# A layer with attention and routed experts: three edits to the order of its instructions

## What is computed

```python
xn = layernorm(x)                                  # no weights
qkv = xn @ W_qkv                                   # 32 query heads, 16 key/value heads of 64
scores = q @ k.T / 8 + slope[h] * (kpos - qpos)    # ALiBi, causal
s = (softmax(scores) @ v) @ W_out                  # back to width 128
logits = xn @ gate_w + gate_b                      # 8 experts, the best 2 of each token
h = gelu(xn @ w1[e] + b1[e])                       # 512 wide, exact gelu
y = sum(softmax(top2)[e] * (h @ w2[e] + b2[e]))    # over the token's two experts
out = x + s * silu(y)
```

## Time and profile before

| | us |
|---|---|
| median of 3 executions | 1218.92 |
| profiled execution | 1220.46 |
| its span, first to last instruction | 1218.7 |
| busy: PE / DVE / ACT / POOL | 1128.5 / 990.2 / 936.7 / 887.8 |
| first half (C0 of body 0 to C0 of body 31) | 55.49 to 557.33 |
| second half from C0 of body 32 | 710.32 |

### The profile page before, as it was taken

One profiled execution on the slowest core, in us unless ns is written; L12 is line 12 of the kernel. 1 busy time (PEld: TensorE's weight loads), 2 busy tenths in 40 slices (PEclk: granted clock), 3 DMA queues, 4 the chain that ended last, 5 costly groups with the idle time before them and its releaser, 6 DMA issues.

```text
span 1218.7 us, 51693 instructions
## 1 busy us (share of the span) xinstructions
PE 1128.5 (93%) x16970; PEld 833.0 (68%) x16970; DVE 990.2 (81%) x3099; ACT 936.7 (77%) x1835; POOL 887.8 (73%) x1064
## 2 busy tenths in 40 slices
PE   2668999999999999999998889999999999999996
PEld 1446666677777777777887657777777777777774
DVE  7787888878888888885776768888888888888883
ACT  4547887878888888887665578888888888888884
POOL 6059988888888888886000048888888888888895
PEclk8579999999999999999999999999999999999998
DMA  8425755655555555556335355555555555555554
GB/s 258 161 53 102 132 127 120 135 116 130 131 127 128 129 127 128 130 133 101 87 90 107 74 137 126 124 127 123 122 122 123 120 122 124 125 124 122 122 122 71
DMA packets 267956, 148.74 MB, mean 122 GB/s; under 512 B 173154, under 2 KB 256450, under 8 KB 267204
## 3 DMA queue, kind: packets, MB, share of 16 engines
q1 hardware_dynamic: 263476, 138.72, 51.3%
q0 software_dynamic: 4096, 8.40, 2.3%
q10 hardware_dynamic: 272, 0.13, 0.0%
HBM read 15.76 MB, written 16.78 MB: 27 GB/s over the span
## 4 chain that ended last, share of the span: by engine, by line
PE 64%; POOL 16%; issue 6%; DVE 4%; ACT 2%; DMA 1%; SPq 1%; POOLq 0%; ACTq 0%; DVEq 0%
POOL t_lo L812 11%; PE ps L965 10%; PE ps L937 7%; PE ps L871 7%; PE ps L872 6%; PE ps L873 6%; PE outs L997 6%; PE ps L969 5%; PE outs L1001 5%; PE outs L999 5%; PE ps L966 3%; PE ps L974 2%; ACT stage L1266 1%; POOL y_now L806 1%; PE outs L872 1%
## 5 line engine op out<-in xcount | busy, mean ns | idle before, releaser
L812 POOL TENSOR_TENSOR t_lo<-stage 128x512 f16<-128x512 f32 x640 | 652.2, 1038 | 120.4 <-ACT stage L1266 118.6
L1548 DVE CUSTOM_DVE_ANT_0 stage<-ps,kmask 128x512 bf16<-128x512 f32 (+3 forms) x1024 | 451.7, 487 | 111.0 <-PE ps L937 96.9
L1266 ACT ACTIVATE stage<-ps,slope 128x512 f32<-128x512 f32 (+1 forms) x768 | 440.4, 618 | 90.1 <-PE ps L974 77.9
L965 PE MATMUL ps<-q_st,k_st 128*128 128x256 f16 (+3 forms) x1024 | 299.7, 303 | 10.5 <-issue 5.0
L997 PE MATMUL outs<-v_sp,stage 128*128 128x65 f16 x2560 | 265.1, 195 | 9.6 <-POOL t_lo L812 7.8
L999 PE MATMUL outs<-v_sp,stage 128*128 128x64 f16 x2560 | 263.9, 194 | 0.0
L1001 PE MATMUL outs<-v_sp,t_lo 128*128 128x65 f16 x2560 | 263.8, 194 | 0.0
L997 PEld LDWEIGHTS outs<-v_sp,stage 128*128 128x128 bf16 x2560 | 235.5, 98 | 34.0 <-issue 14.5
L999 PEld LDWEIGHTS outs<-v_sp,stage 128*128 128x128 bf16 x2560 | 236.0, 99 | 0.0
L1001 PEld LDWEIGHTS outs<-v_sp,t_lo 128*128 128x128 f16 x2560 | 235.6, 98 | 0.0
L966 PE MATMUL ps<-q_st,k_st 128*128 128x128 f16 x1024 | 223.7, 218 | 0.0
(11 more groups left out here) (218 smaller groups left out, 2698.2 us busy)
## 6 DMA issues: line engine op xcount, KB each, us to landing
q_st<-stage SPq DMA_DIRECT2D x256, 128.0 KB, 2.4
k_st<-stage SPq DMA_DIRECT2D x128, 128.0 KB
q_st<-stage SPq DMA_DIRECT2D x256, 64.0 KB, 2.0
k_st<-stage SPq DMA_DIRECT2D x128, 64.0 KB
slot_y<-stage SPq DMA_DIRECT2D x40, 128.0 KB, 2.0
X<-in_L_attn_inputs SPq DMA_DIRECT2D x8, 512.0 KB, 7.5
slot_x<-att SPq DMA_DIRECT2D x2, 2048.0 KB, 8.9
wx_raw<-in_L_ffn_w SPq DMA_DIRECT2D x64, 64.0 KB
```

The source lines that it names most:

```text
L812: pool.tensor_tensor(t_lo[r], t_p[r], upper(t_p[r]), ALU.subtract).then_inc(s[f"lo{u % NG}"], 1)
L965: pe.matmul(d, k[:, 0, at], q[:, 0, seen], start=(c0 == 0), stop=False, skip_group_check=True)
L1266: e = act.activation(t_p[r][:, c0:c1], S_ps[u % 2][:, c0:c1], ACT.Exp, scale=slope[:, bass.ds(pair_index(n) * 2 * SLOTS + sl * 2 + h, 1)])
L1548: ins = dve.tensor_tensor_reduce(junk[h][:, c0:c0 + w], M_ps[h][:, c0:c0 + w], kmask[:, SEQ - w:SEQ], -1.0 / 1024, 3e38, ALU.add, ALU.min, ...
```

## The change

Five things are edited, all of them places in an order; no arithmetic is changed, apart from where an operation stands.

- **Routing.** `choose` now has four pieces (the last three are one), `route` ten; they stand further apart, the last `route` piece (the weights of the two experts) behind the last body of the first half. `ranks` on TensorE and `keep_ranks` on ScalarE move from the window before body 0 into it. GpSimd's nine pieces are spread over bodies 0 to 3.
- **Sends.** The first sending body is 4 instead of 2. Five bodies send twice (6, 9, 12, 15, 18) instead of three (4, 7, 10), and the second tile's second DMA goes out one body later. Through `max(TWICE)` the written-out bodies reach to 19 instead of 11.
- **Between blocks.** The four projections stand two parts apart, the two windows take 12 parts each, and `FILL_AT` gives the rounds and their peaks places of their own.
- **Last body.** GpSimd's adds for bodies 62 and 63 and the last step of a pair stand behind the last lower part; SyncE's store of that pair behind the last transposes.

```diff
@@ one_window, FIRST_ONES
-                if part is not None and at * part[1] // 100 != part[0]:
+                if part is not None and FILL_AT.get(name, at) * part[1] // 100 != part[0]:
-        FIRST_ONES = {"DVE": [("B1", 0), ("B3", 0), ("B5", 0), ("B7", 0), ("B9", 0), ("B11", 0),
-                              ("B3", 1), ("B5", 1), ("B7", 1), ("B9", 1), ("N0", 0), ("B11", 1),
-                              ("N0", 4), ("N0", 6), ("N0", 8)],
-                      "PE": [("C0", 0)], "ACT": [("C1", 0)],
-                      "POOL": [("L1", 0), ("L3", 0), ("L5", 0), ("L7", 0), ("L9", 0), ("L1", 1), ("L4", 1), ("L6", 1), ("L9", 1)]}
-        CHOICES = 6
+        FIRST_ONES = {"DVE": [("B1", 0), ("B5", 0), ("B9", 0), ("Q0", 1), ("B9", 1), ("B11", 1), ("B5", 2), ("B9", 2), ("B5", 3), ("B9", 3),
+                              ("B5", 5), ("B9", 5), ("B5", 6), ("A1", HALF - 1)],
+                      "PE": [("S2", 0)], "ACT": [("E3", 0)],
+                      "POOL": [("L3", 0), ("L7", 0), ("L1", 1), ("L5", 1), ("L9", 1), ("L3", 2), ("L7", 2), ("L3", 3), ("L7", 3)]}
+        CHOICES = 4
+        FILL_AT = {"M0": 84, "B0": 85, "B1": 85, "M1": 95, "M2": 18, "B4": 18, "B5": 18, "M3": 35, "B6": 35, "B7": 35, "M4": 51,
+                   "B8": 51, "B9": 51, "M5": 68, "B10": 68, "B11": 68}
@@ begin_half
-            names = AHEAD[engine_name]
-            for i, name in enumerate(names):
-                if i == b:
+            apart = 2
+            for i, name in enumerate(AHEAD[engine_name]):
+                if apart * i == b:
                     tasks[name[0]](lo, lo % UNROLL, int(name[1:]))
-            b -= len(AHEAD["PE"])
-            each = (blocks - len(AHEAD["PE"])) // 2
+            b -= apart * len(AHEAD["PE"])
+            each = (blocks - apart * len(AHEAD["PE"])) // 2
@@ sends
-        FIRST_SENT, TWICE = 2, (4, 7, 10)
+        FIRST_SENT, TWICE = 4, (6, 9, 12, 15, 18)
@@ GpSimd
             def send(n, par, k):
-                for t, at, _ in sent_with(n, par):
+                sent = [(t, at) for t, at, _ in sent_with(n, par) if (k, at) != (1, UNROLL)]
+                if k == 1 and isinstance(n, int) and n - 1 in TWICE:
+                    sent.append(sent_with(n - 1, 0)[0][:2])
+                for t, at in sent:
...
+            LAST_ADDS = (BODIES - 2, BODIES - 1)
+            def add_or_leave(n, par, _):
+                if not isinstance(n, int) or n not in LAST_ADDS:
+                    add_expert(n, par, 0)
...
             leave_bodies("POOL", fetches, HALF, BODIES)
+            for n in LAST_ADDS:
+                add_expert(n, n % UNROLL, 0)
+            finish(HALF + LAST - 1, 1, 2)
@@ SyncE
+            run_bodies(sp, "SP", {**stacks, "H": hand_out_or_leave}, HALF, BODIES)
             leave_bodies("SP", stacks, HALF, BODIES)
+            hand_out(HALF + LAST - 1, 1, 0)
@@ TensorE
-            enter_bodies("PE", {**tasks, "Y": ranks}, 0, HALF)
-            run_bodies(pe, "PE", tasks, 0, HALF)
+            enter_bodies("PE", tasks, 0, HALF)
+            run_bodies(pe, "PE", {**tasks, "Y": ranks}, 0, HALF)
@@ ScalarE
-            enter_bodies("ACT", {**tasks, "W": weights_hi, "Y": keep_ranks}, 0, HALF)
+            enter_bodies("ACT", {**tasks, "W": weights_hi}, 0, HALF)
             act.wait_ge(s["consts"], 9)
-            run_bodies(act, "ACT", {**tasks, "W": weights_hi, "R": send_hi}, 0, HALF)
+            run_bodies(act, "ACT", {**tasks, "W": weights_hi, "R": send_hi, "Y": keep_ranks}, 0, HALF)
@@ VectorE: the weights of the two experts, route piece 6 before, the last piece now
-            leave_bodies("DVE", tasks, 0, HALF, late=LATE_O)
+            leave_bodies("DVE", {**tasks, "Y": lambda k: route(k - CHOICES)}, 0, HALF, late=LATE_O)
```

More of the change, by code:

```diff
@@ L650, in hand_out, with hand_out_or_leave @@
                     sp.dma_start(ot[:, bass.ds(t, 2), :], X[:, bass.ds(t, 2), :]).then_inc(s["outd"], 16)
-            run_bodies(sp, "SP", {**stacks, "H": hand_out}, HALF, BODIES)
+            def hand_out_or_leave(n, par, _):
+                if not isinstance(n, int) or n != HALF + LAST - 1:
+                    hand_out(n, par, 0)
+            run_bodies(sp, "SP", {**stacks, "H": hand_out_or_leave}, HALF, BODIES)
             leave_bodies("SP", stacks, HALF, BODIES)
+            hand_out(HALF + LAST - 1, 1, 0)
             sp.wait_ge(s["fin_last"], 1)
@@ L856, in finish, with finish_or_leave @@
                     pool.tensor_tensor(tiles_of(X, t), tiles_of(X, t), m, ALU.add).then_inc(s["fin"], 1)
-            fetches = {"L": lo_part, "I": fetch_ready, "D": fetch, "G": add_expert, "U": finish}
+            def finish_or_leave(n, par, k):
+                if not isinstance(n, int) or (n, k) != (HALF + LAST - 1, 2):
+                    finish(n, par, k)
+            fetches = {"L": lo_part, "I": fetch_ready, "D": fetch, "G": add_or_leave, "U": finish_or_leave}
             enter_bodies("POOL", fetches, HALF, BODIES)
@@ L1323, in keep_ranks @@
                 act.copy(total_of, ps[4][:, RANK + NT * E:RANK + (NT + 1) * E]).then_inc(s["kept"], 1)
-            enter_bodies("ACT", {**tasks, "W": weights_hi, "Y": keep_ranks}, 0, HALF)
-            act.wait_ge(s["gap"], 1)
-            act.activation(top[:, 5, :], top[:, 4, :], ACT.Exp).then_inc(s["topexp"], 1)
+                act.wait_ge(s["gap"], 1)
+                act.activation(top[:, 5, :], top[:, 4, :], ACT.Exp).then_inc(s["topexp"], 1)
+            enter_bodies("ACT", {**tasks, "W": weights_hi}, 0, HALF)
             act.wait_ge(s["consts"], 9)
-            run_bodies(act, "ACT", {**tasks, "W": weights_hi, "R": send_hi}, 0, HALF)
+            run_bodies(act, "ACT", {**tasks, "W": weights_hi, "R": send_hi, "Y": keep_ranks}, 0, HALF)
             leave_bodies("ACT", {**tasks, "W": weights_hi, "R": send_hi}, 0, HALF)
@@ L1473, in choose @@
                     small(dve.scalar_tensor_tensor(out=L2, in0=one1, scalar=-3e38, in1=L, op0=ALU.mult, op1=ALU.add))
-                elif k == 3:
+                else:
                     of_value(L2, top[:, 2, :])
-                elif k == 4:
                     of_index(top[:, 3, :])
-                else:
                     small(dve.tensor_tensor(one2, ev, over_e(top[:, 3, :]), ALU.is_equal))
@@ L1523, in route @@
                 elif k == 6:
+                    small(dve.tensor_tensor(ended, block_no[:, :, :], end.unsqueeze(1).to_broadcast([P, NBLK, E]), ALU.is_ge))
+                elif k == 7:
+                    small(dve.tensor_reduce(blk_f[:, :], ended, AX_X, ALU.add))
+                    small(dve.tensor_scalar(blk_f[:, :], blk_f[:, :], E - 1.0, None, ALU.min))
+                elif k == 8:
+                    small(dve.tensor_tensor(eights[:, :, :], eights[:, :, :],
+                                            blk_f[0:1, :].rearrange("p (a b) -> p a b", b=WORD), ALU.mult))
+                    small(dve.tensor_reduce(word_f[:, :], eights[:, :, :], AX_X, ALU.add))
+                    dve.tensor_copy(blk_word[:, :], word_f[:, :]).then_inc(s["numbered"], 1)
+                else:
                     dve.wait_ge(s["topexp"], 1)
@@ L1527, in route @@
                     small(dve.tensor_tensor(top[:, 7, :], top[:, 6, :], top[:, 5, :], ALU.mult))
-                elif k == 7:
-                    small(dve.tensor_tensor(ended, block_no[:, :, :], end.unsqueeze(1).to_broadcast([P, NBLK, E]), ALU.is_ge))
-                    small(dve.tensor_reduce(blk_f[:, :], ended, AX_X, ALU.add))
-                    small(dve.tensor_scalar(blk_f[:, :], blk_f[:, :], E - 1.0, None, ALU.min))
-                else:
-                    small(dve.tensor_tensor(eights[:, :, :], eights[:, :, :],
-                                            blk_f[0:1, :].rearrange("p (a b) -> p a b", b=WORD), ALU.mult))
-                    small(dve.tensor_reduce(word_f[:, :], eights[:, :, :], AX_X, ALU.add))
-                    dve.tensor_copy(blk_word[:, :], word_f[:, :]).then_inc(s["numbered"], 1)
             def peaks(n, par, j):
```

## The result

The changed kernel takes 1212.92 us (median of 4 runs, 1212.06 to 1213.68), the kernel before 1219.74 beside it (4 runs, 1217.27 to 1220.98). The ratio is 0.9944, 95% interval 0.9922 to 0.9965. So it is 6.8 us faster, where 1199.0 us and a gain of 20 were forecast, and the time lies above the range of 1190 to 1211. A second set of runs on another occasion gave 0.9947 (0.993 to 0.9963). The profiled execution took 1212.31 us, its span is 1210.6.

A forecast was written before the change was run, and what follows sets the result against it. TensorE holds 64% of the wait chain, with a floor of 15.10 us per body, so only the excess could fall. Terms sum to -19.9 from 1220.46, giving 1200.6, less 1.54 to the median: 1199.0 us, range 1190 to 1211.

The forecast's parts named there:

- Term 2: Bodies 1 to 5: moved routing pieces cost time, sends and lumps that leave save more; -1.9 us in sum.
- term 6: Route's last piece, 2.70 us, behind body 31: mostly hidden before the first gelu is done; +0.8 us (0 to 2.7).
- rival D: Small TensorE waits in bodies 1 to 5 keep its clock at 1.2 GHz; two such bodies give 1229 us; chance 0.04.
- rival A: VectorE pays in full for moved pieces, at the entry and in bodies 1 to 5; 1207.5 us; chance 0.18.
- term 1: Entry to C0 of body 1: choose and route pieces leave, ranks move into body 0; -4.7 us.
- term 3: Bodies 6 to 10: the lumps and doubled sends that stood there go, stretches fall to 15.10; -7.0 us.
- Doubled sends: Five bodies that send two tiles cost 0.4 us each, mostly fitting GpSimd's free time; +2.0 us (0 to 17).
- rival B: Each doubled send costs as much as now, 17 us in place of 2; 1214 us; chance 0.10.
- Bodies written out: Bodies 12 to 19 leave the loop, saving 0.58 us for each of four turns; -2.3 us, possibly 0.
- terms 7 and 8: Between blocks: ScalarE's store wait shrinks, -3.3 us; rounds two parts apart, -3.0; later Q0 delays C0, +0.6.

The follow-up runs named there:

- both_early: Changed kernel with route's pieces 7 and 8 moved from bodies 5 and 6 to behind B3 of bodies 8 and 9; 1206.5 us, ratio 0.9885.
- eights_n0: Changed kernel with only route's piece 8 back at its earlier place, behind N0 of body 8; 1206.5 us, ratio 0.9894.
- spread: Changed kernel with one routing lump less in each of bodies 0 to 2, sends from body 5, six double sends, bodies written out to 23; 1199.99 us, ratio 0.9831.
- unroll_only: Kernel before with nothing but bodies 12 to 19 written out in place of four loop turns; 1222.88 us, ratio 1.0018.
- port4: Kernel without the layer: small VectorE instructions beside GpSimd runs of seven; held to the run's end behind indirect DMAs, 0.25 to 0.74 us without.

## Why the prediction was wrong, point by point

Against one profile of each kernel, in us:

| term | forecast | measured |
|---|---|---|
| 1 entry to C0 of body 1 | -4.7 | -6.1 |
| 2 bodies 1 to 5 | -1.9 | +8.7 (84.75 to 93.40) |
| 3 to 5 bodies 6 to 19 | -7.3 | -6.8 |
| 6 to 8 body 31 to C0 of body 33 | -4.9 | -2.7 (171.13 to 168.40) |
| 9 last body | -1.1 | -1.6 |

Term 2 misses by 10.6 us, the other terms together by 0.8. Of the 10.6, body 5 has 6.8 (22.15 against 15.4), body 2 has 2.9, body 4 has 1.4, and body 3 came out 0.5 better.

**The step that failed is term 2, in "Body 5 gets the last small piece: +0.3 (0 to 1.2)"**, and "in two lumps: 16.0" for body 4. A small piece was priced by its place among VectorE's instructions and by its durations in the trace, not by what GpSimd does beside it, and no wait of TensorE for the Q0 behind it is in the sum. It cost 7.0 us in body 5: 4.7 us in which TensorE waited for Q0, and the rest, 2.4 us, at TensorE's lower clock. In body 4 the TENSOR_SCALAR cost 1.3 (17.45 against 16.17 with it moved). both_early and eights_n0 show it: with both moved, or the product alone, the kernel is at 1206.5 us, inside the range. With both_early's bodies 4 and 5, 16.17 and 15.10, the forecasts of 16.0 and 15.4 stand.

The reading of the lump of 2.70 us failed in the same way. More than half of it was time in which its instructions were held: behind body 31 the same three take 0.17, 0.35 and 0.19 us, so the whole piece is 0.8 us long there, and term 6 could cost no more than that, not 2.7.

**Bodies 1 and 2.** Body 1 came as forecast in one profile (19.46 against 19.5) and not in the other (21.75), so that agreement is partly luck. Body 2 did not: 19.22 and 19.14, not 16.3. TensorE's waits in the changed kernel:

```profile
89.26 0.39 PE L900 MATMUL ps<-xT_hi,wk_hi 128*128 128x512 f16 x1 [2.34 <-DVE stage L1584]
97.53 0.40 PE L977 MATMUL ps<-ident,spread 128*128 128x128 f16 x4 [1.77 <-DVE stage L1584]
116.75 0.40 PE L977 MATMUL ps<-ident,spread 128*128 128x128 f16 x4 [1.93 <-DVE stage L1584]
```

I had counted that its two sends leave, but not that TensorE's waits in body 1 (2.3 and 1.8 us for Q0) would bring the lower clock again: 0.91 over body 2, where before had 1.00, with TensorE busy for 16.93 us. That is rival D's mechanism in small, some 1.8 us over the floor of 15.10; the remainder is mostly the third wait, again for Q0.

The pieces themselves also grew, by the mechanism of body 5 in small. One instruction of `route`, in body 0 of the kernel before and in body 2 of the changed one:

```profile
81.42 0.19 DVE L1516 TENSOR_SCALAR slot_bits<-slot_of 128x64 uint32<-128x64 uint32 x1
111.22 1.05 DVE L1543 TENSOR_SCALAR slot_bits<-slot_of 128x64 uint32<-128x64 uint32 x1
```

The instructions that moved from body 0 to bodies 1 and 2 took 5.6 us in all before (3.4 and 2.2) and 8.2 in the changed kernel (4.3 and 3.9), held up to one GpSimd instruction at a time. Term 2 counted 3.6 and 2.3. That the 1.6 us more in body 2 make up its third wait is likely and was not tested.

VectorE set the length of both bodies, which is what rival A says of them; its other half, term 1 at -1, did not come (-6.1). The two bodies and the held product together carried the time past A's 1207.5.

**Doubled sends.** 15.53 and 15.65 against 15.10: 0.4 to 0.55 each, where 0.4 was forecast. The -7.0 of term 3 had some luck in it: 1.9 us of it is the 18.47 of body 10, which took 16.53 in the second profile of before. With the sends one body later (spread) the stretch of 15.53 moved from body 7 to body 8, though body 7 itself, the first to send twice there, has 15.72. No stretch comes near the 3.4 of rival B: it is out.

**Bodies written out.** The -2.3 was right for the bodies (-1.7 alone) and wrong for the kernel: by itself the edit is 2.2 us slower (0.6 to 3.8). The profile puts the loss between the halves, where TensorE waits for the loads of expert inputs. SyncE issues the same DMAs in the same order there, 1.3 to 2.7 us later against C0 of body 31. But the changed kernel, with the same bodies written out, issued them as early as before in one execution and 1.6 us later in another. So it is not shown that the edit makes the loads late, only that the kernel is slower with it; the cause stays open. The prediction gave no chance to an effect outside the bodies.

**Between the halves.** Undone in the changed kernel, terms 7 and 8 are worth 7 us (5.7 forecast), 2.7 for SyncE's part (3.3). Between the profiles of before and after only 1.6 to 5.8 of it show, depending on which of the two of each are compared; that the written-out bodies take the rest back would fit unroll_only and is not shown. The C0 behind the later Q0 waits 1.1 us, where 0.6 (0 to 1.2) was put for it.

**Last body.** -1.1 forecast, 1.0 to 1.2 by the run that undid it. The -1.6 in the table holds 0.4 to 0.6 us more, which that run does not account for.

## What to carry to other kernels

Before you move a small VectorE instruction whose tensors all lie in SBUF, look at GpSimd in the same microseconds. If it is of a kind that is held (here a product of two tensors, TENSOR_SCALAR, CAST), then beside a run without gaps that follows an indirect DMA it costs what is left of that run, whatever its size. A small instruction that takes 0.84 us where others of its size take 0.18 is a warning of a price that depends on its place; see what ends with it. And judge an edit by making it or undoing it alone, over the whole kernel: the written-out bodies gained 1.7 us in place, and the kernel was 2.2 us slower.

## What was not expected of the hardware

- VectorE's product of two 1x40 SBUF tensors took 0.18 to 0.20 us outside GpSimd's runs and 0.47 to 1.01 in runs without an indirect DMA before them. In runs with one it took what was left: 0.84 and 1.06 us in the last instruction of a run, 3.67, 4.78 and 7.34 us earlier in it. TENSOR_SCALAR (1.84 and 3.73) and CAST (4.72) behave alike; TENSOR_REDUCE (0.49) and operands in PSUM (0.69) do not. The rule of the Trainium skill, page "SBUF — State Buffer", that one instruction is waited for, agrees with the runs without a DMA and not with the others.
- GpSimd pays little itself: its runs of seven took 7.01 to 7.03 us in port4 with a held VectorE instruction beside them.
- The stage between the halves differs by 3 us between two executions of the same kernel (171.1 and 174.2), and single stretches at the start by up to 2.3 (body 1 of the changed kernel: 19.46 and 21.75).
